# A gated cross-attention and mixture-of-experts block: the maximum's chunk beside the scores, and the first matmuls of four expert passes in half precision pairs

## The reference

```python
def block(x, ctx):
    n = layernorm(x)
    q, k1, v1 = n @ Wq1, n @ Wk1, n @ Wv1
    k, v = concat(k1, ctx @ Wk2), concat(v1, ctx @ Wv2)       # 768 keys
    attn = softmax(q @ k.T * 64 ** -0.5)                      # per batch row and head
    x = x + tanh(g_xattn) * ((attn @ v) @ Wo + bo)
    n = layernorm(x)
    w, i = top_k(n @ gate_w + gate_b, 2); w = softmax(w)
    out = gelu(n @ ws1 + bs1) @ ws2 + bs2                     # shared expert
    for e in range(8):
        out += combine[:, e] * (gelu(n @ w1[e] + b1[e]) @ w2[e] + b2[e])
    return x + tanh(g_ffn) * out
```

## Time and profile before

| | us |
|---|---|
| median of 3 runs | 157.04 (156.72 to 157.09) |
| the profiled execution | 156.95 |
| its span, first to last instruction | 155.1 |
| TensorE busy | 143.9 (93%) |
| ScalarE busy | 115.1 (74%) |
| GpSimd busy | 107.9 (70%) |
| VectorE busy | 103.5 (67%) |

### The profile page before, as it was taken

One profiled execution on the slowest core, in us unless ns is written; L12 is line 12 of the kernel. 1 busy time (PEld: TensorE's weight loads), 2 busy tenths in 40 slices (PEclk: granted clock), 3 DMA queues, 4 the chain that ended last, 5 costly groups with the idle time before them and its releaser, 6 DMA issues.

```text
span 155.1 us, 4389 instructions
## 1 busy us (share of the span) xinstructions
PE 143.9 (93%) x1804; PEld 111.4 (72%) x1804; DVE 103.5 (67%) x215; ACT 115.1 (74%) x191; POOL 107.9 (70%) x95
## 2 busy tenths in 40 slices
PE   7789699979899999999898799999999999999992
PEld 5434354547566667657686698999999999989992
DVE  0779898888777686887763363834643779896631
ACT  3466789998988988887859988645567598968720
POOL 5506999777676667857798878965398089688730
PEclk9999999999999999999999999999999999999999
DMA  5679996000000000000000000030000000100001
GB/s 139 200 268 276 277 351 208 1 4 0 4 2 8 0 4 0 4 0 4 0 4 0 4 0 4 16 119 0 4 0 0 6 2 9 29 0 0 4 0 34
DMA packets 10253, 7.71 MB, mean 50 GB/s; under 512 B 1101, under 2 KB 8442, under 8 KB 10234
## 3 DMA queue, kind: packets, MB, share of 16 engines
q1 hardware_dynamic: 10234, 7.44, 15.8%
HBM read 7.18 MB, written 0.26 MB: 48 GB/s over the span
## 4 chain that ended last, share of the span: by engine, by line
PE 73%; DVE 10%; ACT 9%; issue 2%; DMA 2%; POOL 1%; SPq 0%; DVEq 0%; ACTq 0%
PE banks L1279 12%; PE banks L991 10%; PE banks L993 9%; PE banks L992 9%; PE banks L1242 5%; DVE part L821 4%; PE banks L1170 4%; ACT prob L646 3%; PE banks L1172 3%; PE banks L1171 3%; PE banks L1120 3%; PE banks L1190 2%; ACT v_hi L635 2%; DMA wf<-in_ctx_dram 2%; ACT p_hi L654 2%
## 5 line engine op out<-in xcount | busy, mean ns | idle before, releaser
L554 POOL TENSOR_TENSOR p_lo<-prob,p_hi 128x1024 f16<-128x1024 f32 x23 | 49.0, 2133 | 15.7 <-ACT p_hi L654 15.5
L710 ACT ACTIVATE prob<-banks,b1T 128x256 f32<-128x256 f32 x72 | 28.4, 475 | 12.8 <-PE banks L993 9.3
L646 ACT ACTIVATE prob<-banks 128x1024 f32<-128x1024 f32 x24 | 24.6, 1023 | 8.1 <-PE banks L1138 8.1
L821 DVE TENSOR_REDUCE part<-banks 128x2 f32<-128x1024 f32 (+1 forms) x24 | 29.0, 1216 | 1.1 <-PE banks L1093 1.0
L654 ACT ACTIVATE p_hi<-prob 128x1024 f16<-128x1024 f32 x24 | 25.4, 1057 | 0.8
L569 POOL TENSOR_TENSOR k_both<-prob,k_both 128x1024 f16<-128x1024 f32 x8 | 17.6, 2194 | 4.2 <-ACT k_both L718 3.2
L1279 PE MATMUL banks<-ring,prob 128*128 128x128 f32 x160 | 19.6, 276 | 0.0
L1170 PEld LDWEIGHTS banks<-v_hi,p_hi 128*128 128x128 f16 x192 | 17.4, 98 | 2.9 <-issue 2.5
L1170 PE MATMUL banks<-v_hi,p_hi 128*128 128x65 f16 x192 | 19.2, 195 | 0.0
L1171 PE MATMUL banks<-v_lo,p_hi 128*128 128x64 f16 x192 | 19.1, 193 | 0.0
L1172 PE MATMUL banks<-v_hi,p_lo 128*128 128x65 f16 x192 | 19.1, 194 | 0.0
(11 more groups left out here) (155 smaller groups left out, 343.8 us busy)
## 6 DMA issues: line engine op xcount, KB each, us to landing
ring<-in_L_ffn_w_dram SPq DMA_DIRECT2D x16, 256.0 KB, 5.3
wf<-in_ctx_dram SPq DMA_DIRECT2D x2, 256.0 KB, 5.3
ring<-in_L_xattn_Wk_dram SPq DMA_DIRECT2D x2, 256.0 KB, 4.7
ring<-in_L_xattn_Wv_dram SPq DMA_DIRECT2D x2, 256.0 KB, 7.1
ring<-in_L_ffn_ws_dram SPq DMA_DIRECT2D x2, 256.0 KB, 6.7
x_sb<-in_x_dram SPq DMA_DIRECT2D x1, 256.0 KB, 3.0
ring<-in_L_xattn_Wq_dram SPq DMA_DIRECT2D x1, 256.0 KB, 5.0
wo<-in_L_xattn_Wo_dram SPq DMA_DIRECT2D x1, 256.0 KB, 7.8
```

Of the source, the lines that this page charges most:

```text
L554: nc.gpsimd.tensor_tensor(p_lo[:, u % RINGP, :, :].rearrange("p a n -> p (a n)"), prob[:, u % RINGE, :], p_hi[:, u % RINGP, :, :].rearrang ...
L646: nc.scalar.activation(prob[:, u % RINGE, :], units(u).rearrange("p a n -> p (a n)"), ACT.Exp, scale=DH ** -0.5 / S_SCORE).then_inc(exp_do ...
L710: nc.scalar.activation(hid[:, k % NHID, c * T1:(c + 1) * T1], span(2 * (k % 2), HC * T1)[:, c * T1:(c + 1) * T1], ACT.Gelu, bias=b1T[:, e ...
L821: nc.vector.tensor_reduce(dst, src, AX_X, ALU.max).then_inc(part_done, 1)
```

## The change

TensorE does a step's chunk right behind its scores, and the chunk of step -1 moves to step 0, behind scores 0. VectorE reduces the chunk, from step 0 on, ahead of tails, shift_out and the values' reciprocal; for steps below 0 its order stays, so that the reduction of chunk (1, 0) keeps its place in step -1, ahead of the items' remainders.

Passes 1 to 4 do their first matmul in pairs like the others. Of these four experts' first matrices GpSimd makes hi in steps 7, 10, 13 and 16, behind `p_lo` of the unit, and VectorE makes lo at the end of steps 9, 12, 15 and 18 (`expert_lo`). `split_after_use` goes. The second matrices of passes 1 to 7 are split by ScalarE and VectorE at the steps where those of passes 2 to 8 were.

```diff
-H32 = (1, 2, 3, 4)
-EARLY = 1 + len(H32)
-H32_SPLIT = [(1, 0), (2, 0), (1, 1), (3, 0), (4, 0)]
-H32_STEP = [FFN0 + 2, FFN0 + 3, FFN0 + 5, FFN0 + 6, FFN0 + 7]
+EARLY = 5
+EARLY_HI_STEP = (7, 10, 13, 16)
+EARLY_LO_STEP = (9, 12, 15, 18)
-W2_STEP = {2: FFN0 + 2, 3: FFN0 + 3, 4: FFN0 + 6, 5: FFN0 + 7, 6: FFN0 + 8, 7: FFN0 + 9, 8: FFN0 + 10}
+W2_STEP = {1: FFN0 + 2, 2: FFN0 + 3, 3: FFN0 + 6, 4: FFN0 + 7, 5: FFN0 + 8, 6: FFN0 + 9, 7: FFN0 + 10}
...
+        def early_part(j):
+            return 2 if j < 1 else 1
...
             def early_hi(j):
                 pool.wait_ge(ld_f[j], 32)
-                nc.gpsimd.tensor_tensor(flat(wf[:, 0, EORDER[j], :, :]), flat(ring_f(j)),
-                                        c_sw[:, :].broadcast_to([P, 2 * 512]), ALU.mult).then_inc(e_hi, 1)
+                n = early_part(j)
+                nc.gpsimd.tensor_tensor(flat(wf[:, 0, EORDER[j], 0:n, :]), flat(ring_f(j)[:, 0:n, :]),
+                                        c_sw[:, :].broadcast_to([P, n * 512]), ALU.mult).then_inc(e_hi, 1)
-            def split_after_use(m):
...
-                if i in H32_STEP:
-                    split_after_use(H32_STEP.index(i))
+                if i in EARLY_HI_STEP:
+                    early_hi(EARLY_HI_STEP.index(i) + 1)
...
+            def chunk_maximum(p, c):
+                part_max(p, c)
+                if c == UPP - 1:
+                    whole_max(p)
+                if (p, c) == (0, UPP - 1):
+                    item_of(len(PRE) - 1)
...
                 if i >= 0:
                     for n in items_at(i):
                         item_of(n)
+                if i >= 0 and chunk_of(i) is not None:
+                    chunk_maximum(*chunk_of(i))
                 for b, s in tail_of(i - 1):
                     tail(b, s)
...
                     normalise(values_of(i))
-                if chunk_of(i) is not None:
...
+                if i < 0 and chunk_of(i) is not None:
+                    chunk_maximum(*chunk_of(i))
...
+                if i in EARLY_LO_STEP:
+                    j = EARLY_LO_STEP.index(i) + 1
+                    dve.wait_ge(e_hi, j + 1)
+                    expert_lo(j, slice(0, early_part(j))).then_inc(ed_lo, 1)
...
                 if 0 <= i < NU:
                     scores(i)
+                if i == 0:
+                    max_chunk(*chunk_of(-1))
+                if i != -1 and chunk_of(i) is not None:
+                    max_chunk(*chunk_of(i))
...
-                    elif k in H32:
-                        pe.wait_ge(ld_f[k], 32)
+                    elif k < EARLY:
+                        pe.wait_ge(ed_lo, k)
...
-                        if k in H32:
-                            last = nc.tensor.matmul(dst, ring_f(k)[:, 0, cols], x2T[:, tok], start=True, stop=True)
-                        else:
-                            last = three(dst, (wf[:, 0, e, 0, cols], wf[:, 1, e, 0, cols]),
-                                         (x2h[:, 0, tok], x2h[:, 1, tok]))
+                        last = three(span(2 * (k % 2), HC * T1)[:, c * T1:(c + 1) * T1],
+                                     (wf[:, 0, e, 0, cols], wf[:, 1, e, 0, cols]),
+                                     (x2h[:, 0, tok], x2h[:, 1, tok]))
...
                 if shift_of(i) is not None:
                     shift_row(shift_of(i))
-                if chunk_of(i) is not None:
-                    max_chunk(*chunk_of(i))
```

More of the change, by code:

```diff
@@ L360, in block_kernel @@
         e_scaled, e_hi, e_lo = sem("e_scaled"), sem("e_hi"), sem("e_lo")
-        h32_hi, h32_scaled, h32_lo = sem("h32_hi"), sem("h32_scaled"), sem("h32_lo")
+        ed_lo = sem("ed_lo")
         hh_act = sem("hh_act")
@@ L712, in _ @@
                                              bias=b1T[:, e * HC + c:e * HC + c + 1],
-                                             scale=1.0 if k in H32 else 1.0 / (S_ACTV * S_W)).then_inc(gelu_done, 1)
+                                             scale=1.0 / (S_ACTV * S_W)).then_inc(gelu_done, 1)
                     if k in SPLIT_HID:
@@ L1228, in _ @@
                         pe.wait_ge(e_lo, 1)
-                    elif k in H32:
-                        pe.wait_ge(ld_f[k], 32)
+                    elif k < EARLY:
+                        pe.wait_ge(ed_lo, k)
                     elif k < NE:
                         pe.wait_ge(w1_lo, k - EARLY + 1)
-                    elif k - NE in H32:
-                        pe.wait_ge(h32_lo, H32_SPLIT.index((k - NE, 0)) + 1)
                     if k % NE == 0:
@@ L1239, in _ @@
                         cols = slice(c * P, (c + 1) * P)
-                        dst = span(2 * (k % 2), HC * T1)[:, c * T1:(c + 1) * T1]
-                        if k in H32:
-                            last = nc.tensor.matmul(dst, ring_f(k)[:, 0, cols], x2T[:, tok], start=True, stop=True)
-                        else:
-                            last = three(dst, (wf[:, 0, e, 0, cols], wf[:, 1, e, 0, cols]),
-                                         (x2h[:, 0, tok], x2h[:, 1, tok]))
+                        last = three(span(2 * (k % 2), HC * T1)[:, c * T1:(c + 1) * T1],
+                                     (wf[:, 0, e, 0, cols], wf[:, 1, e, 0, cols]),
+                                     (x2h[:, 0, tok], x2h[:, 1, tok]))
                         if c % 2 == 1:
@@ L1268, in _ @@
                             pe.wait_ge(w2_lo, W2_LATE.index(k % NE) + 1)
-                        elif (k % NE, 1) in H32_SPLIT:
-                            pe.wait_ge(h32_lo, H32_SPLIT.index((k % NE, 1)) + 1)
                         pe.wait_ge(hl_done, hid_splits(k))
```

## The result

| | before | after |
|---|---|---|
| median of 22 runs each, us | 156.86 (156.40 to 158.08) | 157.26 (156.95 to 159.16) |
| ratio, 95% interval | | 1.0052 (1.0028 to 1.0076) |
| profiled execution (span), us | 156.95 (155.1) | 157.06 (155.3) |
| scores of steps 0, 9, 12, 15, 18, 22 start at | 17.32, 45.56, 54.47, 63.46, 72.95, 83.79 | 16.95, 46.27, 55.56, 64.85, 75.16, 85.76 |

The forecast was 155.6 and faster; the time is 157.26 and slower, within the range. Of the 22 executions of after, 13 had a mean granted clock of 0.999 or 1.00 and took 156.95 to 157.37 (median 157.11, so 0.25 slower than before); nine had 0.988 or 0.989 and took 158.21 to 159.16. Part of the 0.40 between the medians is thus a second effect, treated behind the experiments. The profiles of before and after are both of executions at full clock.

A forecast was written before the change was run, and what follows sets the result against it. TensorE was taken as the bound, busy for 93% of the span. The terms -1.6 - 1.4 + 0.88 + 0.9 + 1.2 + 0.5 - 1.84 sum to -1.36, from 156.95 to 155.6 us; range 154.2 to 158.4.

The forecast's parts named there:

- the walk: Attention cycle traced: each start is the later of its engine's previous instruction and its inputs; errors of 0.1.
- part 1: TensorE in attention: two changes of matmul shape per step instead of four, 0.2 saved in eight steps, -1.6 us.
- part 4: VectorE's shift behind the chunk's reduction: TensorE waits in steps 6, 9, 12 and 15, +0.9 us; copy term separate.
- The waits before the chunks of steps 7 and 19: TensorE's waits for VectorE's reduction of the chunk before go away, 0.7 each, -1.4 us.
- The start: Chunk (1, 0) behind scores 0 delays its reduction, k lo and TensorE's key item, with nothing absorbing it: +0.88 us.
- The term of +1.2 for the copy of step 17: Step 17: the first output tile's copy stands behind the reduction on VectorE, delaying TensorE's transposes, +1.2 us gross.
- Remainders: Four expert remainders on VectorE in attention: cost 0 in steps 9, 12 and 15, +0.5 us in step 18.
- the rule of first come: VectorE remainders against GpSimd subtractions: whoever starts second waits; VectorE first by 0.2 in steps 9, 12 and 15.
- Pairs in passes 1 to 4: Experts' first matmuls in half precision pairs take 1.31 instead of 1.81 or 1.73 each, -1.84 us.
- The rival with blocked remainders: Steps 9, 12, 15: remainders second to GpSimd; one blocked 157.0, two 158.4, three 159.7; chances 0.16 (one or two), 0.10 (three).
- The rival of the better case: Start's 0.88 absorbed, step 18's remainder first (0.5), or shift not waiting: 154.7, or 154.2 with both; chance 0.20.
- The rival that ended on the slower side: Passes 1 to 4: the experts' part gains nothing, wide matmuls having hidden ScalarE or VectorE work, 157.4 us; chance 0.08.

The follow-up runs named there:

- the experiment: Changed kernel with chunk (1, 0) put back in step -1, ahead of scores 0: 156.29 us, ratio 0.9955 to the kernel before.
- the mended kernels: Keys' hi ahead of `p_hi` on ScalarE: on the changed kernel 154.72 us; start back and fourth remainder in step 21 too, 153.29; chunk's move alone, start unmoved, 154.94.

## Why the prediction was wrong

**The step that failed is in the walk behind parts 1, 2 and 4: the chunk was treated as ready as soon as TensorE comes to it.** The walk followed the chunk's result (reduction, shift, copy) and its banks, but not its own input. For c=1 and c=2 that is right. For c=0 the keys' hi is 0.7 late. What the runs showed: TensorE waits 0.79 by the starts (0.56 to 0.63 of recorded idle time) in steps 8, 11 and 14, and the cycle is 9.29 where the walk has 8.81 (8.91, less 0.4 of part 1, plus 0.3 of part 4). The three waits are 2.4. They hide the 0.8 that part 4 put at steps 9, 12 and 15, so 1.5 to 1.6 is left, and that is the whole error: scores 22 start 1.97 later and were forecast at +0.48, and the experts are within 0.1. Everything else in the sum came nearly as forecast. The starts of scores in after, less those before, were +0.75 in step 1, +0.73 in step 5, +0.12 in step 8, +0.71 in step 9, +1.09 in step 12, +1.39 in step 15, +1.17 in step 17, +2.21 in step 18, +1.51 in step 20 and +1.97 in step 22.

By its parts:
1. Changes of shape, -1.6: right. Scores 10, 13 and 16, behind steps without a wait, start 0.21 or 0.22 sooner against the scores before them than they did. With the wait mended the cycle is 0.32 shorter than before, 0.4 forecast, and 0.09 of wait is left in it.
2. The waits before the chunks of steps 7 and 19, -1.4: gone, and scores 8 and 20 gain 0.70 each, as forecast.
3. The start, +0.88: items 0.75 later (20.43 against 19.68), 0.8 by the experiment.
4. The shift behind the reduction, +0.9: the chain was right (5.26 for 5.25), but the waits of steps 9, 12 and 15 did not show, since TensorE had already lost 0.79 to the keys' hi. No run shows this term by itself: in the mended kernels the swap on ScalarE shortens the shift's chain by 0.7. A wait of 0.24 in step 3 was not foreseen. The term of +1.2 for the copy of step 17 was right: scores 18 start 1.04 later against scores 17 than before, after part 1's 0.2.
5. Remainders: right, by the rule of first come. VectorE was first by 0.37 (forecast 0.2) in steps 9, 12 and 15, second in step 18 at 2.52 (2.6), which cost 0.46 (0.5). GpSimd's products took 1.03 to 1.04 (1.1).
6. Pairs in passes 1 to 4, -1.84: 1.31 each, -1.8 in all.

The rival with blocked remainders was right as a mechanism and not decisive: the move of the reduction, which was booked as a cost alone, is also what lets VectorE be first. The rival of the better case failed: the start was not absorbed, and the remainder of step 18 was blocked. The rival that ended on the slower side was the wrong one; what came true had no place among the cases, so the chance of 0.62 for faster was too high.

The Trainium skill (SBUF — State Buffer, "Who interferes with whom") has VectorE with two SBUF inputs and a GpSimd instruction that reads SBUF excluding each other. The runs agree in both orders: 2.13 instead of 0.68 for the one that came 0.55 late, 2.31 instead of 2.13 for GpSimd when it was second.

## What to carry to other kernels

When an instruction is moved forward on an in-order engine, write down every semaphore that it waits for, its inputs' too, with the time at which each is given; what stood between was cover for the latest of them, and ready work queued behind it now waits as well. When such a wait appears, look first at the order on the engine that makes the input: here two instructions swapped on ScalarE were worth 2.4 us, and two on VectorE 0.6 to 0.7 (152.56 against 153.20 at full clock and 153.29 over all). Try the halves of a change together as well as alone: where two engines exclude each other, the part that looks like a cost can be what puts the other in front.

## What was not expected of the hardware

- With a gap of 1.3 us on TensorE early in the kernel (until 19.6 us), 9 of 22 executions had a mean granted clock of 0.988 or 0.989 and took 1.1 to 2.1 us longer than the median of the others. Two profiles of such executions, of kernels with the same gap, show a granted clock of 0.50 for about 3 us from 21 us on, one to two us behind the gap. With ten matmuls in the gap, 1.26 us of work, none of 12 executions did this.
- In the kernel with the late fourth remainder alone, VectorE's remainder in step 21 took 1.42, between 0.68 and 2.13, when it started at 87.64, 1.26 after a subtraction on GpSimd (86.38); it ended at 89.06, 0.55 after the 2.13 of that one. In the kernel with the experts' part alone the remainder of step 9 ended 0.55 after it too (51.63 and 51.08). In both, the one that came second waited for the rest of the first, not for a fixed time.
